# Down products three slots behind instead of two, their low halves written over the activation, and two setup transpositions moved from slot 5 to slot 17

## What is computed

```python
    g = jnp.einsum('bsd,edf->ebsf', h, Wg)
    u = jnp.einsum('bsd,edf->ebsf', h, Wu)
    expert_outs = jnp.einsum('ebsf,efd->ebsd', jax.nn.silu(g) * u, Wd)
    expert_output = jnp.einsum('be,ebsd->bsd', gating_probs, expert_outs)
```

## Time and profile before

| | |
|---|---|
| median of 3 runs | 474.82 us (471.68 to 476.14) |
| the profiled execution, its own time | 470.62 us |
| its span in the profile | 468.8 us |
| PE, DVE, ACT, POOL busy | 432.4, 334.4, 282.0, 185.5 us |
| mean granted TensorE clock | 0.972 of full speed |

### The profile page before, as it was taken

The page is one execution under the profiler, slowest core; times in us unless marked ns, Lnnn a source line. Parts: engine busy times, 40 slices in busy tenths (PEclk is TensorE's granted clock), DMA queues, the critical chain, the costliest instruction groups (busy, mean ns, idle before and its releaser), DMA issues.

```text
span 468.8 us, 7759 instructions
## 1 busy us (share of the span) xinstructions
PE 432.4 (92%) x2280; PEld 324.5 (69%) x2280; DVE 334.4 (71%) x589; ACT 282.0 (60%) x572; POOL 185.5 (40%) x235
## 2 busy tenths in 40 slices
PE   7799699699999999999999999999999977988896
PEld 3568578578678787867878787788788554554453
DVE  4887467586777779777767987686687757567763
ACT  5757367575465657645565755555555646567684
POOL 0857567573223222332224222334377324234440
PEclk9999799899999999999999999999999989789999
DMA  5524214210002020000111000001221714665630
GB/s 161 157 74 149 91 52 129 78 37 3 1 1 90 1 68 1 22 0 0 53 36 35 32 0 1 1 27 42 69 70 34 171 50 122 175 156 148 152 104 24
DMA packets 27891, 30.69 MB, mean 65 GB/s; under 512 B 4276, under 2 KB 22296, under 8 KB 27864
## 3 DMA queue, kind: packets, MB, share of 16 engines
q1 hardware_dynamic: 26664, 29.99, 22.5%
q0 software_dynamic: 768, 0.28, 0.3%
q10 hardware_dynamic: 432, 0.10, 0.1%
HBM read 22.73 MB, written 7.35 MB: 64 GB/s over the span
## 4 chain that ended last, share of the span: by engine, by line
PE 59%; DVE 14%; issue 9%; DMA 6%; ACT 6%; POOL 5%; POOLq 1%; DVEq 0%; ACTq 0%; SPq 0%
PE acc_ps L520 7%; DVE act_lo L1101 6%; PE g_ps L520 5%; PE acc_ps L521 5%; PE g_ps L522 5%; PE g_ps L521 5%; PE acc_ps L522 5%; PE u_ps L520 5%; PE u_ps L522 5%; PE u_ps L521 5%; DVE act_p L1097 4%; DMA w_raw<-in_L_cond_Wu 4%; ACT act_p L818 2%; DMA squares<-in_squares 1%; DMA q_blocks<-max_rows 1%
## 5 line engine op out<-in xcount | busy, mean ns | idle before, releaser
L818 ACT ACTIVATE act_p<-g_ps 128x512 f32<-128x512 f32 x144 | 86.0, 597 | 127.9 <-PE g_ps L522 112.4
L1097 DVE TENSOR_TENSOR act_p<-act_p,u_ps 128x512 f32<-128x512 f32 x144 | 98.5, 684 | 71.4 <-PE u_ps L522 45.7
L1101 DVE TENSOR_TENSOR act_lo<-act_p,act_hi 128x512 fp32r<-128x512 f32 x144 | 122.8, 853 | 0.2 <-ACT act_hi L823 0.2
L1303 POOL TENSOR_TENSOR xg_lo<-xg,xg_hi 128x512 fp32r<-128x512 f32 x35 | 49.6, 1418 | 155.1 <-ACT xg_hi L828 155.1
L823 ACT ACTIVATE act_hi<-act_p 128x512 fp32r<-128x512 f32 x144 | 89.8, 624 | 2.0 <-DVE act_p L1097 1.8
L520 PE MATMUL acc_ps<-act_hi,w_split 128*128 128x512 f32 x144 | 62.0, 431 | 15.9 <-DVE act_lo L1101 15.8
L520 PE MATMUL g_ps<-x_hi,w_split 128*128 128x512 f32 (+1 forms) x144 | 57.6, 400 | 0.6 <-DVE x_lo L1130 0.6
L521 PE MATMUL acc_ps<-act_lo,w_split 128*128 128x512 f32 x144 | 57.1, 397 | 0.0
L522 PE MATMUL acc_ps<-act_hi,w_split 128*128 128x512 f32 x144 | 56.9, 395 | 0.0
L520 PE MATMUL u_ps<-xg_hi,w_split 128*128 128x512 f32 x144 | 56.8, 394 | 0.1
L521 PE MATMUL g_ps<-x_lo,w_split 128*128 128x512 f32 (+1 forms) x144 | 56.8, 394 | 0.0
(11 more groups left out here) (190 smaller groups left out, 679.8 us busy)
## 6 DMA issues: line engine op xcount, KB each, us to landing
k_blocks<-k_rows SPq DMA_DIRECT2D x32, 96.0 KB
q_plain<-q_rows SPq DMA_DIRECT2D x8, 384.0 KB
q_blocks<-q_rows SPq DMA_DIRECT2D x32, 96.0 KB
k_plain<-k_rows SPq DMA_DIRECT2D x8, 384.0 KB
w_raw<-in_L_cond_Wg SPq DMA_DIRECT2D x8, 256.0 KB, 2.7
w_raw<-in_L_cond_Wu SPq DMA_DIRECT2D x8, 256.0 KB, 2.7
w_raw<-in_L_cond_Wd SPq DMA_DIRECT2D x8, 256.0 KB, 2.9
q_rows<-rows_hi SPq DMA_DIRECT2D x16, 128.0 KB
```

The lines of the kernel that those rows point to most:

```text
L818: activation(act_p[k % 3][:], g_ps[k % 3][:], ACT.Silu).then_inc(silu_done, 1)
L1097: tt(act_p[k % 3][:], act_p[k % 3][:], u_ps[k % 3][:], ALU.mult).then_inc(prod_done, 1)
L1101: tt(act_lo[k % 3][:], act_p[k % 3][:], act_hi[k % 3][:].bitcast(F32), ALU.subtract).then_inc(act_lo_done, 1)
L1303: tt(xg_lo[e % 3][:], xg[:].rearrange("p b s -> p (b s)"), xg_hi[e % 3][:].bitcast(F32), ALU.subtract)\
```

## The change

1. Buffers: `act_p`, `act_hi`, `act_lo` had three buffers each, nine tiles of 128x512. Now there are four `act_hi` and four `act_p`; the four `act_lo` lie on the addresses of the four `act_p`. So `split_act` writes the low half over the activation.
2. PE: D follows three slots behind. Slot k issues D(k-3); the last three of a tile stand in slots 0 to 2 of the next, and after the last tile three are left.
3. ACT: silu(k) waited for split_act(k-3); it now waits for D(k-4). round_act(k) waited for D(k-3); it now waits for D(k-4).
4. DVE: `add_experts` moves from slot 1 to slot 2. `sum_self` of a natural step of slot s moves from DVE's slot s+2 to slot s+4.
5. The setup step moves from slot 5 to slot 17 of tile 0, on PE and DVE.
6. POOL's `multiply_self` is written at the head of the following slot instead of the end of a slot; its place in POOL's list stays. SP's list stays, too.

```diff
-FIRST_SLOT = {4: ("bias", 0, 0), 5: ("setup", 0, 0), 6: ("side", 0, 0), 8: ("query", 0, 0)}
+FIRST_SLOT = {4: ("bias", 0, 0), 6: ("side", 0, 0), 8: ("query", 0, 0)}
 FIRST_SLOT |= {10 + 2 * _b: ("natural", 0, _b) for _b in range(TB)}
+FIRST_SLOT |= {17: ("setup", 0, 0)}
+ACTS = 4
+BEHIND = 3
...
-        act_p = [sb(f"act_p{n}", [128, N]) for n in range(3)]
-        act_hi = [sb(f"act_hi{n}", [128, N], F32R) for n in range(3)]
-        act_lo = [sb(f"act_lo{n}", [128, N], F32R) for n in range(3)]
+        act_hi = [sb(f"act_hi{n}", [128, N], F32R) for n in range(ACTS)]
+
+        with ExitStack() as products:
+            act_p = [products.enter_context(nc.sbuf_tensor(f"act_p{n}", [128, N], F32)) for n in range(ACTS)]
+        act_lo = [sb(f"act_lo{n}", [128, N], F32R) for n in range(ACTS)]
...
-                if k >= 2:
-                    down_product(0, k - 2)
+                if k >= BEHIND:
+                    down_product(0, k - BEHIND)
...
-                down_product(*((t, k - 2) if k >= 2 else (t - 1, SLOTS - 2 + k)))
+                down_product(*((t, k - BEHIND) if k >= BEHIND else (t - 1, SLOTS - BEHIND + k)))
...
-            for k in range(2):
-                down_product(NT - 1, SLOTS - 2 + k)
+            for k in range(SLOTS - BEHIND, SLOTS):
+                down_product(NT - 1, k)
...
             def silu(t, k):
-                wait(act, act_lo_done, t * SLOTS + k - 2)
+                wait(act, down_done, t * SLOTS + k - 3)
                 act.wait_ge(g_written, t * SLOTS + k + 1)
...
             def round_act(t, k):
-                wait(act, down_done, t * SLOTS + k - 2)
+                wait(act, down_done, t * SLOTS + k - 3)
                 act.wait_ge(prod_done, t * SLOTS + k + 1)
...
-                for kind, f, b in first_at(k - 2):
+                for kind, f, b in first_at(k - 4):
                     if kind == "natural":
                         sum_self(f, b)
...
-                    for kind, f, b in next_at(k - 2, t + 1):
+                    for kind, f, b in next_at(k - 4, t + 1):
                         if kind == "natural":
                             sum_self(f, b)
...
-                if k == 1:
+                if k == BEHIND - 1:
                     add_experts(t - 1)
```

More of the change, by code:

```diff
@@ L627, in down_product @@
                 pe.wait_ge(act_lo_done, t * SLOTS + k + 1)
-                last = three(acc_ps[:], w_hi[:, e, 2, chunk], w_lo[:, e, 2, chunk], act_hi[k % 3][:], act_lo[k % 3][:],
+                last = three(acc_ps[:], w_hi[:, e, 2, chunk], w_lo[:, e, 2, chunk], act_hi[k % ACTS][:], act_lo[k % ACTS][:],
                              start=(k == 0), stop=(k == SLOTS - 1))
@@ L815, in silu @@
             def silu(t, k):
-                wait(act, act_lo_done, t * SLOTS + k - 2)
+                wait(act, down_done, t * SLOTS + k - 3)
                 act.wait_ge(g_written, t * SLOTS + k + 1)
-                activation(act_p[k % 3][:], g_ps[k % 3][:], ACT.Silu).then_inc(silu_done, 1)
+                activation(act_p[k % ACTS][:], g_ps[k % 3][:], ACT.Silu).then_inc(silu_done, 1)
             def round_act(t, k):
-                wait(act, down_done, t * SLOTS + k - 2)
+                wait(act, down_done, t * SLOTS + k - 3)
                 act.wait_ge(prod_done, t * SLOTS + k + 1)
-                activation(act_hi[k % 3][:], act_p[k % 3][:], ACT.Identity).then_inc(act_hi_done, 1)
+                activation(act_hi[k % ACTS][:], act_p[k % ACTS][:], ACT.Identity).then_inc(act_hi_done, 1)
             def round_xg(t, e):
@@ L1096, in product @@
                 dve.wait_ge(silu_done, t * SLOTS + k + 1)
-                tt(act_p[k % 3][:], act_p[k % 3][:], u_ps[k % 3][:], ALU.mult).then_inc(prod_done, 1)
+                tt(act_p[k % ACTS][:], act_p[k % ACTS][:], u_ps[k % 3][:], ALU.mult).then_inc(prod_done, 1)
             def split_act(t, k):
                 dve.wait_ge(act_hi_done, t * SLOTS + k + 1)
-                tt(act_lo[k % 3][:], act_p[k % 3][:], act_hi[k % 3][:].bitcast(F32), ALU.subtract).then_inc(act_lo_done, 1)
+                tt(act_lo[k % ACTS][:], act_p[k % ACTS][:], act_hi[k % ACTS][:].bitcast(F32), ALU.subtract).then_inc(act_lo_done, 1)
             def add_experts(t):
@@ L1316, in _ @@
                 e, c = divmod(k, FC)
+                for kind, f, b in first_at(k - 2):
+                    if kind == "natural":
+                        multiply_self(f, b)
                 if e + 1 < NE and c == 1:
@@ L1322, in _ @@
                     split_part(3 * (e + 1) + c)
-                for kind, f, b in first_at(k - 1):
-                    if kind == "natural":
-                        multiply_self(f, b)
                 for kind, f, b in first_at(k + PICK_AHEAD):
```

## The result

The changed kernel takes 460.15 us (median of 4 runs, 457.77 to 460.65) against 474.12 us (4 runs, 471.68 to 476.14) for the kernel before: a ratio of 0.971, interval 0.965 to 0.977. A fifth execution of the changed kernel, outside these four, took 463.0 us. The profiled execution took 457.77 us, 12.85 us less than that of before, where 12.9 had been forecast; its span is 455.8 us.

A forecast was written before the change was run, and what follows sets the result against it. PE was taken as the bound, mostly waiting for DVE's low half. Gains of 9.5 us (tile 0) and 5.6 us (tiles 1 to 3), less 2.2 for a clock dip, gave 12.9 off 474.82: 461.9 us, range 456 to 469.

The forecast's parts named there:

- Tiles 1 to 3: Ten short waits of down products go: 3.1 us of idle time plus restarts, 5.6 us gained.
- The new wait at the adapter's product: Slot 3 of the next tile: the product comes 0.1 to 0.3 us late, three times, counted zero.
- The debt at the end: Last tile: one down product less done (0.68 us) falls due after U(35), hidden by a 0.8 us wait, counted zero.
- Start of tile 0: Slots 0 to 8: the query step starts at 32.6 to 32.9 instead of 35.48, taken as 2.6 us.
- The first long wait: Tile 0, U(16): the wait passes to the up product, 2.4 us instead of 3.9; G(17) comes 6.7 us earlier.
- The second: Tile 0, U(28): PE waits 2.5 us for xg_lo; the query step for tile 1 starts 7.2 us earlier.
- The DVE-bound stretch: End of tile 0, up to the diffusion: DVE starts 0.9 us earlier; G(31) starts 9.5 us earlier.
- One clock dip: Tile 0: of two possible dips behind the two long waits, one was assumed, taking 2.2 us off the gain.
- The sign by which tile 0's slots should end some 10 us earlier: Check on the new profile: tile 0's 36 slots end some 10 us earlier.
- the overlay: Rival: writing over the operand slows the split, decided from 1.36 us on; 491 us, chance 0.05.
- that the transfers don't move: Rival: the late weight part lands when it did, so both long waits end at old times; 467 us, chance 0.12.
- that the lead is used up: Rival: looped tiles pay 1 us each at the adapter's product and both dips stay; 472 us, chance 0.07.

The follow-up runs named there:

- a_behind_only: Changed kernel with the setup step back in slot 5 and the reductions back two slots behind their natural step: 461.78 us, ratio 0.975.
- e_stores_later: Changed kernel with SP's six stores after each query step issued behind two weight parts more: 457.99 us, ratio 0.965.
- i_overlay_only: Kernel before with only the low half written over the activation, in the three buffers there were: 472.35 us, ratio 0.998.
- h_sum_only: Kernel before with the reductions alone moved to four slots behind: 469.47 us, ratio 0.995.
- j_stores_spread: Changed kernel with the six stores after each query step issued two behind each of three weight parts: 453.82 us, ratio 0.960.
- k_spread_before: Kernel before with only the six stores issued two behind each of three weight parts: 464.15 us, ratio 0.980.
- c_sum_back: Changed kernel with the reductions alone put back to two slots behind: 460.95 us, ratio 0.975.

## Why the prediction was right, and where it wasn't

The forecast of 462 us holds (460.15), by 13.0 us of span against 12.9. Its mechanism stood: the waits for the low half go, and in tile 0 they pass to the up product. That the sum came out to 0.1 us is luck, since two of its terms in tile 0 were off in opposite directions.

- **Tiles 1 to 3, 5.6 us: measured 252.3 - 246.3 = 6.0.** All five kernels without the third slot need 252.2 to 252.3 us there and all six of the experiments and the change with it 246.2 to 246.3, whatever else they change: the third slot alone makes this term. The waits said 3.1; the rest comes of restarts, as in the row at 287.40, where a start is late by more than the idle time. By the Trainium skill (Perfetto Trace Analysis, section Identifying the Most-Contended Engine) busy share is a poor measure of how near TensorE is to its limit, and the runs agree: PE's idle time gives 3.1 us, the time between marks 6.0.
- **The new wait at the adapter's product, 0.1 to 0.3 us, counted zero:** two of 0.2 us at most. **The debt at the end, counted zero:** the last D wait fell from 0.8 to 0.4, and one D of 0.68 came in; of 13.44 us gained at the start of the last gate product, 13.15 were left at the last down product. So 0.3 us of the debt were paid.
- **Start of tile 0, 2.6 us: measured 1.9** (query step at 33.59). The row at 21.99 tells why: behind the 2.15 us before U(4) the matmuls took 0.63 instead of 0.39 us and came 0.43 apart, until about 25. From U(4) to U(5) it took 4.41 us (21.18 to 25.59), where `a_behind_only` took 2.81: 1.6 us. The side step so starts at 29.02 instead of the 28.1 of the forecast. The forecast had this wait leave the clock alone, as in the earlier trace rows, and in `a_behind_only` it did: the same wait, 2.16 us, and matmuls of 0.39 us behind it. Of the seven kernels with the third slot only that one and `e_stores_later` were spared.
- **The first long wait, 2.4 us at U(16): measured 2.78, for the same `xg_lo`.** G(17) starts 5.4 us earlier, not 6.7: the load came into ACT 1.7 us earlier (49.68 against 51.36) instead of 2.3, and `xg_lo` 1.2 instead of 2.3, since the natural step's multiplication (`stage`), still ahead of it on POOL, took 0.90 us instead of 0.45.
- **The second, 2.5 us at U(28): measured 2.42.** Query step for tile 1 5.8 us earlier, not 7.2.
- **The DVE-bound stretch: G(31) 7.2 us earlier, not 9.5.** This is the term that was mis-sized most. The mechanism held: the diffusion's last part ends at 94.79 + 0.60 = 95.39 and G(31) follows 0.49 later, as I had it. But it ends 5.8 us earlier than in the earlier trace rows, where I had 8.1: 1.4 of the difference is the later query step, and some 0.7 lie in the stretch itself, 13.0 us from 82.39 to 95.39, where I had taken durations over from before. Two DVE instructions grew: the diffusion's scaling of its edge columns took 1.27 us where the kernel before had 0.16, and the first pair of its sums 2.40 where it had 1.39 (the rows of before stand in the last section). Two splits that had taken 1.49 us got shorter, 0.68 and 1.16, which gave part of it back.
- **One clock dip, 2.2 us, taken off: there was none behind either long wait.** The waits of 2.78 and 2.42 us were followed by matmuls of 0.47 and then 0.39 us. The one dip stood at the start, where I had none. So two errors cancelled: 9.5 - 2.2 = 7.3 forecast for tile 0, 7.4 measured, though of this dip and this 9.5 neither came. The sign by which tile 0's slots should end some 10 us earlier failed with them: they ended 7.4 earlier.

Of the rivals, the overlay (split from 1.36 us on) is out by 685 ns in the change and by `i_overlay_only`; that the transfers don't move, by the load at 40.65 instead of 42.39; that the lead is used up, by tiles 1 to 3.

What the prediction didn't ask is how the parts add up. Alone, by one trace each, the third slot gives 2.5 us in tile 0, the reductions 5.5, the setup step nothing (it was 0.8 us longer, `i_overlay_only` 1.1); together they give 7.4. Once the third slot is there, either of the other two moves brings tile 0 from 99.3 to about 95.3 and the second adds 0.6 to 1.2. How these parts divide isn't shown: dips of the clock worth up to 2 us each lie in some of these executions and not in others. What the lists of waits do show is which wait each part touches. The third slot takes every late `act_lo` of tile 0 off PE's path; the reductions' move shortens the two long ones; the setup step's move takes away the wait for the columns, which is 3.3 us only once the third slot is there. Behind the two long waits stands the same late load in every case. With the third slot it ends the wait through `xg_lo`. In `h_sum_only` it does so through ACT, which rounds the weight part first and only then runs the silu that DVE waits for. None of the parts touches the load. `j_stores_spread` and `k_spread_before` do, and this is worth 6.1 us of tile 0 on top of the change and 8.3 without it; the ratios bear it out (0.960 against 0.971, and 0.980 against 1).

Open stays what decides a dip of the clock. In the changed kernel it came behind the wait of 2.15 us at 21.18 and not behind 2.78 us at 53.86. In `a_behind_only` it came behind 1.86 us and not behind 2.16 or 2.71. In `c_sum_back` one stands at 86.28, where no wait was over 2.25 us. In tile 0 of the twelve traces all seven waits of 3.26 us or more were followed by one, and of those between 1.8 and 2.9 us some were and some were not. A fourth slot behind wasn't tried; in tiles 1 to 3 nothing is left for it to win.

## What to carry to other kernels

When a wait is removed, look for the next operand that the same late load makes late, and price what remains by its time, not by the wait that went. Where loads share a queue with stores, count what stands ahead of each load: here two stores behind each load did more for tile 0 (8.3 us in the kernel before) than all the reordering of the engines' work (7.4), and tiles 1 to 3 took as long as before (252.2 against 252.3 us). A stretch bound by one engine shouldn't be moved with its old durations, since its instructions meet other ones of the neighbour engine.

## What the runs showed of the hardware

**A tiny DVE instruction can last as long as its neighbour on POOL.** The scaling of 128x8 elements starts at 85.26 and ends at 86.53; POOL's weight part runs from 84.76 to 86.50. The kernel before had the same instruction while POOL stood idle, in its timeline, together with the pair of sums:

```profile
92.55 0.16 DVE L1008 TENSOR_SCALAR dif_a<-x_in 128x8 f32<-128x8 f32 x1
...
97.25 1.39 DVE L1016 SCALAR_TENSOR_TENSOR dif_a<-dif_a,z_now,dif_b 128x128 f32<-128x128 f32 x2
```

This instruction stands four times in each of the twelve traces. In the six places where POOL's weight part was already running it took 1.25 to 1.27 us and ended with it, in the 42 others 0.16 or 0.17. The Trainium skill (SBUF — State Buffer, section Who interferes with whom) has the two engines share a pair of SBUF ports; a `tensor_scalar` can enter a mode that needs the pair, and then whichever engine issues first keeps it for its whole instruction. The 1.27 against 0.16 us agree, with POOL having started 0.50 us earlier.

**Identical work at the end isn't equally long.** The rest behind the last down product, the same instructions in all twelve kernels, took 99.1 to 105.9 us in the profiled executions; in `e_stores_later` it was 105.9 at a granted clock of 0.83 over this part, in the changed kernel 99.2 at 0.89. A profiled span alone can therefore hide or feign a gain of several us. The marks between stages keep this part out, though not the dips in the stage itself.

**Writing the split's result over its operand costs nothing:** its median is 684 or 685 ns in every kernel, with a buffer of its own or over its input.
